# A two-layer kernel: new step orders in its first layer, and an opening with the weights' product and the first projection ahead

## The chip, the cores and the metric

The kernel runs on one core of a Trainium2 chip. The metric is the device time of one execution in microseconds (us); a run's figure is that of one execution, and several runs are summed up by their median.

The core has five engines that run side by side and meet through semaphores: TensorE (PE) multiplies matrices into PSUM banks, VectorE (DVE) and ScalarE (ACT) work on PSUM and SBUF, GpSimd (POOL) works on SBUF and issues gathers and scatters, SyncE (SP) issues plain DMAs. Each engine does its instructions in the order in which they are written.

## The reference

2048 tokens of width 128 pass through two layers. Layer 0 adds to x an attention through hashed buckets and a mixture of experts in which each token goes to one of eight; layer 1 adds a gated delta-rule attention with two convolutions, and a mixture in which each token goes to two of eight. Both halves of a layer read the same normalised x.

```python
xn = _layernorm(x)
x = x + attn0(xn) + ffn0(xn)
xn = _layernorm(x)
x = x + attn1(xn) + ffn1(xn)
# attn0: Q, K, V = heads(Wq), heads(Wk), heads(Wv)
projK = einsum('bhtd,dp->bhtp', K, planes_T)
logitsK = einsum('bhtlk,kr->bhtlr', tanh(projK) / scale, protos_T)
probsK = softmax(logitsK)
bucket_K, bucket_V = probsK.T @ K, probsK.T @ V
out = softmax(Q @ bucket_K.T / sqrt(dim)) @ bucket_V   # then Wo, bo
```

## The kernel before, in words

**Steps and lists.** The work is cut into named steps. `order_one()` makes one list, ONE, for layer 0, and `order_two()` one, TWO, for layer 1. Every engine walks the same list and does its own share of each step; `late()` shifts some kinds of steps back by a few places for one engine (the tables LATE). So a step's place in the list sets its order on PE, DVE, ACT, POOL and SP at once.

**Layer 0.** Attention is done in eight blocks b of 256 tokens. For a block, PE does `proj` (K's hash projection, L704; ACT takes its tanh), `lmm` (the logits, in two halves i, L729; DVE takes the maximum per group, L1155, and subtracts it, L1160), ACT does `exp`, DVE `fin` (sum, L1166, and reciprocal, L1168) and POOL the product with it (L1767). One round later, by the list ROUND, come `bucket` (L741), `sc` (scores, two halves, L760; DVE takes their maximum, L1185, and writes it negated, L1191), `turn`, `mt` (that maximum turned, L771; DVE adds it to q, L1197), `pair` (scores again, transposed, L782; ACT takes exp), `av` (L793), `half`, `norm` and the output product. `kv` and `q` (L718; DVE copies q, L1147, every second block) make K, V and Q.

The mixture of experts works on 23 tiles of 128 sorted rows: `x0` (SP fetches rows and weights), `h0` (PE turns the rows, L692), `g0` (first product, L826 and L831; ACT's tanh, DVE's product with it, L1258), `y0` (second product, L839; DVE scales it, L1129, and SP stores it). `weighted()` merges these into the attention's list: it gives each attention step a weight from SHARE and places an expert step whenever its share of the weight has passed. Rows get to their expert by `ds` (dispatch: DVE works out the places from the router's choice, L1061 to L1083), `scatter` (POOL, 16 indirect DMAs, L1750, into a buffer that SP has zeroed, L549) and come back by `back0` (POOL, 16 gathers, L1784). The last block's steps and the gathers follow the list LAST; `mom`, `ln1` and `rt` there are the next layer's normalisation, transposes and router.

**PSUM.** Eight banks. lmm, sc and pair take two of three double banks each, g0 takes one; so a step of these waits until the readers of an earlier one are done. `plan_banks` fixes who gets which.

**The opening.** SP loads x in four DMAs and then zeroes the sorted buffer in six. ACT issues eleven DMAs of weights and constants, takes the square root of the variances (L1558), and copies the transposed x from PSUM (L1562). DVE makes the moments of four groups of tokens, then waits for the roots, inverts them (L1103) and normalises (L1033). PE waits for all loads of the semaphore d_wa, transposes (L656), does the router (L666), then `wp` (the product of Wk and the planes, L687), then walks ONE, which begins with proj(0) and ds.

```python
w.wait_ge(d_wa, WA_ALL)              # PE, L678
for c in range(4):
    layernorm("ln0", c, 0)
    if c:
        router(0, rw, "ln0", (c - 1,))
router(0, rw, "ln0", (3,))
step = ("wp",)
```

**Layer 1.** HEAD lists its beginning: projections (`pj`, L883), SP's 64 `stack` DMAs (L630: shifted copies of V, four per stack(c,i), two buffers for c = 0 to 3), `gr` (L917), then the convolutions `fl(c)` (L899) and `fs(c)` (L907), which read stack c; a buffer is filled again once fs(c-2) has read it (`w.wait_ge(psum.full(("fs", c - 2)))`). Then come the recurrence (`r0`, `r1`, `rs`, `ro`, eight steps n, two halves u, L870) and 39 expert tiles (`g1`, L998; `y1`, L1006 and L1007) side by side; the gates in four parts m (`ga`, `ht`, `hid` on PE, L863 and L973, then `lg`, `pr`, `cb`, `nm`), which PLAN['gates'] and PLAN['width'] place; and at the end `back1`: 32 gathers on POOL (L1757), each added by DVE (L1135), through four buffers, merged with the rest of the list after PLAN['back']. A gather on POOL also waits for the last `ro` before it in the list.

Of the kernel before, what the change touches and what calls it, by code (L numbers as in the profile page):

```python
# [129 lines left out]
LAST = ([('back0', 0), ('back0', 1), ('back0', 5), ('back0', 2), ('back0', 3), ('back0', 4), ('back0', 7), ('back0', 6), ('bucket',), ('turn',),  # L130
        ('mom', 0), ('sc', 0), ('sc', 1), ('wc', 0)] + [('back0', n) for n in range(8, 12)] + [('mt',), ('mom', 1), ('ln1', 0), ('pair', 0), ('wc',
        1)] + [('back0', n) for n in range(12, 16)] + [('av', 0), ('rt', 1, 0), ('ln1', 1), ('mom', 2), ('wc', 2), ('rt', 1, 1), ('pair', 1),
        ('ln1', 2), ('av', 1), ('rt', 1, 2), ('half', 0), ('half', 1), ('norm',), ('mom', 3), ('ln1', 3), ('rt', 1, 3)])

HEAD = ([('pj', 1, 0), ('ds', 1)] + [('scatter1', n) for n in range(0, 32)] + [('pj', 1, 1), ('pj', 1, 2), ('pj', 1, 3), ('lh', 1), ('l2', 1),
        ('pj', 0, 1), ('pj', 2, 1), ('beta',), ('pj', 0, 0), ('pj', 0, 2), ('pj', 0, 3), ('kb',), ('lh', 0), ('l2', 0), ('pj', 2, 0), ('pj', 2, 2),
        ('pj', 2, 3)] + [('stack', 0, n) for n in range(0, 4)] + [('stack', 1, n) for n in range(0, 4)] + [('qq',), ('mix',), ('vh',)] + [('gr', n)
        for n in range(0, 8)] + [('din',)] + [('sub', n) for n in range(2, 16)] + [('dout',)])
# [16 lines left out]
def order_one():  # L155

    attn = [("proj", 0), ("ds", 0)]
    for a in range(NB + 1):
# [1743 lines left out]
```

## Time and profile before

| | us |
|---|---|
| three runs | 692.17, 696.11, 697.80 |
| median | 696.11 |
| the profiled execution | 695.66 |
| its span in the profile | 693.9 |
| PE, DVE, ACT, POOL busy | 525.5, 449.6, 208.9, 190.8 |
| layer 0's rounds | about 62 to 319 |
| end of layer 0 (gathers, last block) | about 320 to 369 |

All times of the trace are counted from the start of the span. PE's busy time includes what the pipeline hides; a wait is the idle time of an engine ahead of an instruction, with the engine and line that ended it.

### The profile page before, as it was taken

The numbers are of one execution on the slowest core, as the hardware profiler recorded it, in microseconds if no ns is written. First come the engines' busy times: TensorE is split into PE (matmuls) and PEld (weight loads), VectorE is DVE, ScalarE is ACT, GpSimd is POOL, SyncE is SP. The second block draws the span as 40 slices with busy tenths as digits, with TensorE's granted clock in tenths as the row PEclk, the third lists the DMA queues.
The fourth block names the chain that finished last, engine by engine and source line by source line (L and its number), as shares of the span: only waits on it lengthen the run. The fifth ranks groups of instructions, "written<-read, shape, count | busy, mean of one in ns | idle before, by whom it ended". The sixth has DMA issues, their size and how long they took to land.

```text
span 693.9 us, 17843 instructions
## 1 busy us (share of the span) xinstructions
PE 525.5 (76%) x7491; PEld 359.3 (52%) x7491; DVE 449.6 (65%) x925; ACT 208.9 (30%) x374; POOL 190.8 (27%) x145
## 2 busy tenths in 40 slices
PE   3753698887988788885488998785788789787652
PEld 3531565665756666564244445224777667643422
DVE  6596659595957767792547787990254445828945
ACT  2231144435343434442031441101122233424121
POOL 1184040404021302225831776100000000117641
PEclk9975599999989999999576999996699999997755
DMA  8365022413232332301210114440265665401121
GB/s 239 96 176 168 0 83 64 122 54 107 61 102 77 94 97 65 113 9 21 34 16 1 45 48 122 114 128 21 75 188 174 190 182 159 146 22 43 52 53 30
DMA packets 80975, 62.26 MB, mean 90 GB/s; under 512 B 10080, under 2 KB 74368, under 8 KB 80896
## 3 DMA queue, kind: packets, MB, share of 16 engines
q1 hardware_dynamic: 68832, 51.06, 25.7%
q0 software_dynamic: 4864, 6.30, 3.9%
q10 hardware_dynamic: 7200, 3.77, 1.9%
q8 instruction: 59, 0.97, 0.6%
q14 instruction: 20, 0.16, 0.1%
HBM read 44.10 MB, written 12.32 MB: 81 GB/s over the span
## 4 chain that ended last, share of the span: by engine, by line
PE 39%; DVE 19%; issue 9%; SPq 8%; DMA 5%; POOL 5%; ACT 4%; DVEq 0%; ACTq 0%; POOLq 0%
PE ps L883 6%; SPq L630 4%; PE ps L831 4%; POOL X L1784 4%; DVE small L1155 3%; DVE small L1185 3%; DVE BIG L1160 3%; DMA BIG<-in_wd 3%; PE ps L998 3%; PE ps L782 2%; PE ps L729 2%; DMA BIG<-ys,small 2%; PE ps L839 2%; PE ps L863 1%; SPq L588 1%
## 5 line engine op out<-in xcount | busy, mean ns | idle before, releaser
L1767 POOL TENSOR_TENSOR BIG<-BIG,small 128x2048 f32<-128x2048 f32 x16 | 59.0, 3685 | 204.3 <-DVE small L1168 204.0
L1750 POOL DMA_INDIRECT xs<-BIG,small x48 | 51.9, 1082 | 34.8 <-DVE small L1083 21.0
L1809 POOL TENSOR_TENSOR BIG<-BIG 128x512 f32<-128x512 f32 x4 | 4.8, 1212 | 161.1 <-DVE BIG L1478 161.1
L831 PEld LDWEIGHTS ps<-BIG 128*128 128x128 f32 x368 | 46.5, 198 | 3.7 <-issue 0.6
L831 PE MATMUL ps<-BIG 128*128 128x128 f32 x368 | 46.3, 281 | 0.0
L998 PE MATMUL ps<-BIG 128*128 128x128 f32 x312 | 44.0, 286 | 2.9 <-issue 1.4
L1185 DVE TENSOR_REDUCE small<-ps 128x8 f32<-128x1024 f32 x32 | 37.6, 1217 | 12.9 <-PE ps L760 12.9
L883 PE MATMUL ps<-XT,BIG 128*128 128x512 f32 x96 | 44.2, 620 | 0.0
L1155 DVE TENSOR_REDUCE small<-ps 128x64 f32<-128x1024 f32 x32 | 38.9, 1216 | 7.2 <-PE ps L729 7.2
L1757 POOL DMA_INDIRECT BIG<-ys,small x32 | 31.9, 997 | 41.4 <-DMA ys<-BIG 28.6
L998 PEld LDWEIGHTS ps<-BIG 128*128 128x128 f32 x312 | 39.9, 200 | 3.8 <-issue 1.9
L1160 DVE TENSOR_TENSOR BIG<-ps,small 128x1024 f32<-128x1024 f32 x32 | 39.2, 1225 | 1.1
L1620 ACT ACTIVATE BIG<-ps 128x1024 f32<-128x1024 f32 x32 | 31.0, 1021 | 23.1 <-PE ps L782 23.1
L760 PE MATMUL ps<-BIG 32*128 32x256 f32 x256 | 21.2, 450 | 22.0 <-DVE small L1185 11.0
L1724 ACT ACTIVATE BIG<-ps 128x256 f32<-128x256 f32 x39 | 15.0, 384 | 73.1 <-PE ps L998 73.0
L1166 DVE TENSOR_REDUCE small<-BIG 128x128 f32<-128x2048 f32 x16 | 36.4, 2277 | 0.0
L1129 DVE TENSOR_SCALAR BIG<-ps 128x128 f32<-128x128 f32 x62 | 17.6, 284 | 28.1 <-PE ps L1007 18.3
L1527 DVE SCALAR_TENSOR_TENSOR BIG<-BIG,ps 128x256 f32<-128x256 f32 x39 | 16.3, 419 | 27.9 <-ACT BIG L1724 27.9
L899 PE MATMUL ps<-BIG 128*32 128x512 f32 x256 | 28.3, 593 | 7.4 <-DMA BIG<-BIG 7.4
L1596 ACT ACTIVATE BIG<-BIG 128x1024 f32<-128x1024 f32 x32 | 32.1, 1052 | 0.6 <-DVE BIG L1160 0.6
L1020 DVE STREAM_TRANSPOSE BIG<-BIG 128x512 f32<-128x512 f32 (+2 forms) x25 | 27.2, 1105 | 6.7 <-ACT BIG L1659 5.7
L1640 ACT ACTIVATE BIG<-ps 128x512 f32<-128x512 f32 x23 | 13.7, 598 | 58.2 <-PE ps L831 58.2
(254 smaller groups left out, 1113.3 us busy)
## 6 DMA issues: line engine op xcount, KB each, us to landing
BIG<-in_w SPq DMA_DIRECT2D x23, 512.0 KB, 3.7
BIG<-in_w SPq DMA_DIRECT2D x23, 256.0 KB, 3.8
BIG<-in_wg SPq DMA_DIRECT2D x39, 128.0 KB, 2.2
BIG<-in_wu SPq DMA_DIRECT2D x39, 128.0 KB, 2.6
BIG<-in_wd SPq DMA_DIRECT2D x39, 128.0 KB, 2.7
BIG<-BIG SPq DMA_DIRECT2D x64, 71.4 KB, 2.1
ys<-BIG SPq DMA_DIRECT2D x62, 64.0 KB, 2.2
xs<-BIG SPq DMA_DIRECT2D x14, 256.0 KB, 7.6
```

Of the source, the lines that this page charges most:

```text
L831: t = e.matmul(bank(step)[:, i:i + 128], WT[j % NWT][:, o + i:o + i + 128], XsT[j % 2], start=False, stop=(i == 384))
L883: t = e.matmul(bank(s)[:, :], WC[:, v, j, :], XT[:, 2 * c:2 * c + 2, j:j + 256], start=(j == 0), stop=(j == 3))
L998: t = e.matmul(bank(s)[:, i:i + 128], WT[(NTL[0] + j) % NWT][:, i:i + 128], XsT[(NTL[0] + j) % 2], start=True, stop=True)
L1155: own.after(e.tensor_reduce(MX[v], x, AX, ALU.max))
L1160: e.tensor_tensor(o, x, bc_last(MX[v], 16), ALU.subtract).then_inc(s_empty(step), 1)
L1166: own.after(e.tensor_reduce(zz[i], P[n % 3].rearrange("p (l r) -> p l r", r=16), AX, ALU.add))
L1185: e.tensor_reduce(M16[i][:, 8 * v:8 * v + 8], unit(step).rearrange("p (h s) -> p h s", s=128), AX, ALU.max).then_inc(s_empty(step), 1)
L1596: e.activation(p, p, ACT.Exp).then_inc(exp_done, 1)
L1620: e.activation(ET[2 * u + v], unit(step), ACT.Exp, scale=ISQ8).then_inc(s_empty(step), 1)
L1750: e.indirect_dma_start(XSd[L], bass.IndirectOffsetOnAxis(ap=posi[:, 16 * k + n:16 * k + n + 1], axis=0), xn[:, n, :], None).then_inc(d_sca ...
L1757: e.indirect_dma_start(GA[idx % 4], None, YSd[L], bass.IndirectOffsetOnAxis(ap=posi[:, 16 * k + n:16 * k + n + 1], axis=0)).then_inc(d_ga[ ...
L1767: e.tensor_tensor(v, v, bc_last(zz[i], 16), ALU.mult).then_inc(p_ready, 1)
```

## The change

It reorders steps and rebuilds the opening; what each step computes stays, but for the root of the variance, which is one `pow` of -0.5 on POOL where ACT's Sqrt and DVE's reciprocal stood.

```diff
- 'DVE2': {'nm': 1, ..., 'back1': 4, ..., 'lg': 1, ..., 'y1': 1, ...},
+ 'DVE2': {'nm': 2, ..., 'back1': 6, ..., 'lg': 2, ..., 'y1': 2, ...},
 ROUND:
-        ('q', 0, 1), ('mt', 1), ('fin', 0, 0), ...
+        ('mt', 1), ('q', 0, 1), ('fin', 0, 0), ...
-SHARE = {'lmm': 0.3, 'proj': 4, 'turn': 0.6, 'av': 0.3, 'kv': 4, 'fin': 1.5, 'exp': 1.5, 'sc': 1.5}
+SHARE = {'lmm': 1, 'proj': 4, 'turn': 0.6, 'av': 0.3, 'kv': 4, 'fin': 0.6, 'exp': 4, 'sc': 2.5, 'q': 1, 'bucket': 0.3}
 LAST:
-  ..., ('back0', 6), ('bucket',), ('turn',), ('mom', 0), ('sc', 0), ...
-  ('mt',), ('mom', 1), ('ln1', 0), ('pair', 0), ('wc', 1), back0 12 to 15, ('av', 0), ('rt', 1, 0), ('ln1', 1),
-  ('mom', 2), ('wc', 2), ('rt', 1, 1), ('pair', 1), ...
+  ..., ('back0', 6), ('mom', 0), ('bucket',), ('turn',), ('sc', 0), ...
+  ('mt',), ('mom', 1), ('pair', 0), ('ln1', 0), ('wc', 1), back0 12, 14, 15, ('av', 0), ('rt', 1, 0), ('ln1', 1),
+  ('mom', 2), ('back0', 13), ('rt', 1, 1), ('wc', 2), ('pair', 1), ...
 HEAD:
+  ('stack', 1, 2) behind ('pj', 2, 1), ahead of the other seven of stack 0 and 1
 PLAN:
- 'gates': (23, 41, 48),
- 'width': (19, 15, 11),
+ 'gates': (23, 42, 48),
+ 'width': (19, 15, 14),
 order_one:
-    attn = [("proj", 0), ("ds", 0)]
+    attn = [("proj", 0)]
+            if a == 0 and (name, *rest) == ("lmm", 0):
+                attn += [("ds", 0)]
 plan_banks:
+    psum.plan(("wp",), 5)
-    psum.plan(("wp",), 0)
 SP:
+            e.dma_start(wqT, ...)   # then wkv, woT, bo_b: on d_w0
+            w.wait_ge(d_wa, WA_ALL)
             clear(0)
-            w.wait_ge(d_w0, W0_ALL)
 PE:
-            w.wait_ge(d_wa, WA_ALL)
+            w.wait_ge(d_wp, WP_ALL)
             w.wait_ge(xt_pad, 1)
-            for c in range(4): ... transposes and router
             step = ("wp",)
             e.matmul(bank(step)[:, :], wkN, BPl, ...)
+            layernorm("ln0", 0, 0)
+            project(("proj", 0))
+            for c in range(1, 4):
+                layernorm("ln0", c, 0)
+                router(0, rw, "ln0", (c - 1,))
+            router(0, rw, "ln0", (3,))
+            for s in ONE[1:]:
 DVE:
-            for c in range(4): moments(c)
-            for c in range(4): reciprocal, normalise(XN0, c)
+            for c in range(5):
+                if c < 4: moments(c)
+                if c: normalise(XN0, c - 1)
 ACT (DMAs: ident, wkN, BPl on d_wp; misc, rw; cst; PB):
-            for c in range(4): ACT.Sqrt
-            transposes 0 to 3; isc; wp
+            wp; transpose 0; tanh(("proj", 0)); isc; transposes 1 to 3
 POOL:
+            rstd(0, 1) ... rstd(3, 4)   # e.tensor_tensor(rs[:, sl], rs[:, sl], mhalf, ALU.pow)
             w.wait_ge(d_c, C_ALL)
```

Merged with the new weights, the lists of three rounds read as follows between sc(·,1) and the second pair (before, then after); x0, on SP alone, is left out.

```
round 2   sc1,1 exp2,1 q1,1 y3 mt1 fin2,0 g4 pair1,0 proj3 h5 fin2,1 y4 pair1,1
          sc1,1 exp2,1 y3 g4 mt1 q1,1 h5 fin2,0 pair1,0 proj3 y4 fin2,1 pair1,1
round 3   sc2,1 y6 exp3,1 g7 mt2 fin3,0 h8 pair2,0 proj4 y7 fin3,1 g8 pair2,1
          sc2,1 g7 exp3,1 h8 mt2 fin3,0 pair2,0 proj4 y7 g8 fin3,1 pair2,1
round 5   sc4,1 exp5,1 y13 mt4 fin5,0 g14 pair4,0 proj6 h15 fin5,1 y14 pair4,1
          sc4,1 y13 exp5,1 g14 mt4 h15 fin5,0 pair4,0 proj6 y14 fin5,1 pair4,1
```

At the end of layer 1 the lists read (before, then after):

```
rs5,0 g37 h38 hid1,0 rs5,1 y36 g38 hid1,1 ro5,0 y37 y38 ro5,1 back0 lg1 back1 r06,0 ...
rs5,0 g37 h38 ht1 rs5,1 y36 g38 ro5,0 y37 y38 hid1,0 ro5,1 back0 hid1,1 back1 r06,0 ...
```

## Rows read from the trace of the kernel before

**Rows 1.** Windows: us, busy PE, PEld, DVE, ACT, POOL, clock, DMA, GB/s.
```profile
104.90:140.10 35.20, 29.92 (x316) 21.73 (x316) 25.53 (x36) 14.99 (x24) 7.37 (x2) 1.00 0.28 85
...
618.00:624.00 6.00, 2.67 (x74) 1.32 (x68) 1.19 (x3) 0.28 (x1) 2.50 (x3) 1.00 0.16 42
...
642.00:648.00 6.00, 4.32 (x78) 4.06 (x78) 5.69 (x22) 0.97 (x4) 3.21 (x4) 0.50 0.17 44
```

**Rows 2.** Waits of PE, 72 to 320: us in total, times, longest.
```profile
PE ps L760 <- DVE BIG L1160: 6.8, 4, 2.8
...
PE ps L771 <- DVE BIG L1191: 4.1, 3, 1.5
...
PE ps L771 <- DVE BIG L1147: 2.5, 2, 1.3
PE ps L782 <- DVE BIG L1197: 2.5, 3, 0.9
```

**Rows 3.** Opening in order of time: start, us, engine line, [idle before <-releaser].
```profile
11.26 0.78 PEld L656 LDWEIGHTS ps<-ident,BIG 128*128 128x128 f32 x4 [11.26 <-DMA BIG<-in_PB]
11.29 2.28 PE L656 MATMUL ps<-ident,BIG 128*128 128x128 f32 x8 [11.29 <-DVE BIG L1033]
...
21.54 2.06 PE L687 MATMUL ps<-BIG 128*128 128x512 f32 x2
...
22.46 0.28 DVE L1120 TENSOR_TENSOR small<-ps,BIG 128x128 f32<-128x128 f32 x1
...
24.28 3.78 PE L704 MATMUL ps<-XT,BIG 128*128 128x256 f32 x8 [0.69 <-ACT BIG L1577]
...
28.31 0.42 DVE L1061 TENSOR_TENSOR_SCAN KV<-cst,ps 128x128 f32<-128x128 f32 x1 [3.38 <-PE ps L676]
...
31.87 1.17 POOL L1750 DMA_INDIRECT xs<-BIG,small  x1 [8.68 <-DVE small L1083]
...
47.05 3.93 DVE L1231 TENSOR_SCALAR BIG<-BIG 96x128 f32<-96x128 f32 x1
47.20 3.69 POOL L1767 TENSOR_TENSOR BIG<-BIG,small 128x2048 f32<-128x2048 f32 x1
...
58.52 3.67 POOL L1767 TENSOR_TENSOR BIG<-BIG,small 128x2048 f32<-128x2048 f32 x1 [2.19 <-DVE small L1168]
...
62.24 3.64 PE L741 MATMUL ps<-BIG 128*32 128x256 f32 x32 [15.84 <-POOL BIG L1767]
```

**Rows 4.** End of layer 1 in order of time, columns as in rows 3.
```profile
606.48 1.02 PE L863 MATMUL ps<-XT,BIG 128*128 128x512 f32 x2
...
609.05 1.02 PE L973 MATMUL ps<-BIG 128*128 128x512 f32 x2
...
616.91 0.39 PE L1007 MATMUL ps<-BIG 128*128 128x128 f32 x2
...
620.90 0.99 POOL L1757 DMA_INDIRECT BIG<-ys,small  x1 [28.64 <-DMA ys<-BIG]
```

**Rows 5.** DMA issues by line: KB each, median us from issue to landing.
```profile
cst<-in_cst ACTq DMA_DIRECT2D x1, 204.0 KB, 3.7
```

**Rows 6.** Groups by line: busy, mean ns of one, idle before.
```profile
L1155 DVE TENSOR_REDUCE small<-ps 128x64 f32<-128x1024 f32 x32 | 38.9, 1216 | 7.2 <-PE ps L729 7.2
L1160 DVE TENSOR_TENSOR BIG<-ps,small 128x1024 f32<-128x1024 f32 x32 | 39.2, 1225 | 1.1
```

**Rows 7.** End of layer 0 in order of time, columns as in rows 3.
```profile
352.82 1.63 POOL L1777 TENSOR_TENSOR small<-small 128x4 f32<-128x4 f32 x1
...
354.21 1.15 PE L782 MATMUL ps<-BIG 32*128 32x256 f32 x16
```

**Rows 8.** Chain that ended last, around fs(0) and fl(1); timeline row of fl(1) last.
```profile
438.37 0.59 SPq L630
438.96 0.34 issue
...
441.34 7.08 PE L899 MATMUL ps<-BIG 128*32 128x512 f32 x64 [2.29 <-DMA BIG<-BIG]
```

**Rows 9.** A later projection in order of time, columns as in rows 3.
```profile
87.71 2.00 PE L704 MATMUL ps<-XT,BIG 128*128 128x256 f32 x8
```

More of the change, by code:

```diff
@@ L130 @@
[L130 to L133, printed above, removed]
+SHARE = {'lmm': 1, 'proj': 4, 'turn': 0.6, 'av': 0.3, 'kv': 4, 'fin': 0.6, 'exp': 4, 'sc': 2.5, 'q': 1, 'bucket': 0.3}
@@ new lines @@
+LAST = ([('back0', 0), ('back0', 1), ('back0', 5), ('back0', 2), ('back0', 3), ('back0', 4), ('back0', 7), ('back0', 6), ('mom', 0), ('bucket',),
+        ('turn',), ('sc', 0), ('sc', 1), ('wc', 0)] + [('back0', n) for n in range(8, 12)] + [('mt',), ('mom', 1), ('pair', 0), ('ln1', 0), ('wc',
+        1), ('back0', 12), ('back0', 14), ('back0', 15), ('av', 0), ('rt', 1, 0), ('ln1', 1), ('mom', 2), ('back0', 13), ('rt', 1, 1), ('wc', 2),
+        ('pair', 1), ('ln1', 2), ('av', 1), ('rt', 1, 2), ('half', 0), ('half', 1), ('norm',), ('mom', 3), ('ln1', 3), ('rt', 1, 3)])
@@ L1542, in _ @@
             w = Waits(e)
[L1543 to L1544 removed]
+            e.dma_start(ident[:, :], io["ident"]).then_inc(d_wp, 16)
+            e.dma_start(wkN, io["wkN"]).then_inc(d_wp, 16)
+            e.dma_start(BPl, io["BPl"]).then_inc(d_wp, 16)
             e.dma_start(misc[:, 0:32], io["misc"]).then_inc(d_wa, 16)
             e.dma_start(rw, io["rw"]).then_inc(d_wa, 16)
[L1547 to L1548 removed]
+            e.dma_start(cst[:, 0:408], io["cst"]).then_inc(d_c, 16)
             e.dma_start(PB, io["PB"]).then_inc(d_wa, 16)
[L1550 to L1558 removed]
             def transposed(step, c):
@@ L1569, in sorted_in, with tanh @@
                 e.activation(XsT[J % 2], bank(s)[:, 0:128], ACT.Copy).then_inc(s_empty(s), 1)
-            for c in range(4):
-                transposed(("ln0", c), c)
-            w.wait_ge(d_wa, WA_ALL)
-            e.activation(isc[:, 0:1], lt_b, ACT.Exp).then_inc(isc_ready, 1)
+            def tanh(s):
+                b = s[1]
+                for gg in range(2):
+                    step = s + (gg,)
+                    w.wait_ge(psum.full(step))
+                    if b:
+                        w.wait_ge(psum.full(("lmm", b - 1, 1, 1)))
+                    e.activation(TH[:, 2 * gg:2 * gg + 2, :], bank(step)[:, :].rearrange("p (g t) -> p g t", g=2), ACT.Tanh).then_inc(s_empty(step), 1)
             step = ("wp",)
@@ L1577, in _ @@
             e.activation(Wproj.rearrange("p (g q n) -> p q g n", g=4, q=4), bank(step).rearrange("p (q g n) -> p q g n", q=4, g=4), ACT.Copy).then_inc(s_empty(step), 1)
-            for s in late(ONE, LATE["ACT1"]):
+            transposed(("ln0", 0), 0)
+            tanh(("proj", 0))
+            w.wait_ge(d_wa, WA_ALL)
+            e.activation(isc[:, 0:1], lt_b, ACT.Exp).then_inc(isc_ready, 1)
+            for c in range(1, 4):
+                transposed(("ln0", c), c)
+            for s in late(ONE[1:], LATE["ACT1"]):
                 k = s[0]
                 if k == "proj":
-                    b = s[1]
-                    for gg in range(2):
-                        step = s + (gg,)
-                        w.wait_ge(psum.full(step))
-                        if b:
-                            w.wait_ge(psum.full(("lmm", b - 1, 1, 1)))
-                        e.activation(TH[:, 2 * gg:2 * gg + 2, :], bank(step)[:, :].rearrange("p (g t) -> p g t", g=2), ACT.Tanh).then_inc(s_empty(step), 1)
+                    tanh(s)
                 elif k == "kv":
```

93 lines of the change are left out of this document (44 added, 49 removed).

## The prediction

> **What bounds the kernel now.** I read the windows by stage first, because no engine is full over the whole span. A round of layer 0 (from one bucket step to the next) lasts 35.2 us; PE is busy for 29.9 us of it and DVE for 25.5 [rows 1]. Neither is the limit alone: the loss is PE standing while DVE finishes something. So the waits of PE over the seven rounds come second [rows 2]. The reader is to see there that PE's longest waits stand ahead of sc (L760, for the PSUM banks that lmm's subtraction, L1160, frees) and ahead of mt (L771, for sc's maximum, L1191, and for a copy of q, L1147: 4.1 + 2.5 us), and 2.5 us ahead of pair (L782, for mt's addition, L1197). Third is the opening in order of time [rows 3]: PE stands for 15.84 us before the first bucket step at 62.24, and GpSimd ends that wait. Last is the end of layer 1 [rows 4]: GpSimd's 32 gathers of expert rows start at 620.90, after a wait for the last stored tile, and the chain of the end runs behind them.
>
> **Opening.** Removed: four Sqrt on ACT and four reciprocals on DVE; added: four `pow` on GpSimd. Moved: the product wp and proj(0) go ahead of the router, dispatch (ds) goes behind lmm(0,0), and four weight DMAs go from ACT's queue to SP's, ahead of the six zeroing DMAs. Before, PE starts at 11.26, held by PB, the seventh DMA of ACT's queue [rows 3]. After, it needs only ident, wkN and BPl, that queue's first three. BPl has 256 KB and would be issued at about 1.7; the 204 KB of cst, issued second before, took 3.7 us to land [rows 5], so I take 1.7 + 4.1 = 5.8 for PE's start.
> From there: wp 2.1; the transposes and the router 10.3 (11.29 to wp's start at 21.54 before); proj(0) 3.8, and 0.7 for the copy of XT that it waits for [rows 3]. That is 16.9 us, so the router ends near 22.8, against some 21.6 before. The first maximum and the count take 2.5 (22.46 to 24.93). Now lmm(0,0) stands ahead of ds in DVE's order: two tiles of 1.22 + 1.23, 4.9 us [rows 6]. Then dispatch, 3.6 us to the first scatter (28.31 to 31.87) [rows 3]. Sum: 22.8 + 2.5 + 4.9 + 3.6 = 33.8, against 31.87: the scatters start 1.9 us later.
> What is queued behind them on GpSimd sets the first bucket. Twelve scatters take 31.87 to 47.20, then come the product of fin(0,0), 3.69, and four scatters, and fin(0,1) starts at 58.52, having waited 2.19 us for DVE [rows 3]. DVE now reaches fin(0,1) 2 to 3 us earlier, since its idle 3.38 us before dispatch are filled with lmm(0,0). So the 1.9 us eat most of the 2.19 us of waiting, and the bucket stays at about 62.2: **0 us**, although proj(0) is ready 10 us earlier. From both sides: -4 if every landing is earlier than taken, +3 if PE starts at 8.
> The new `pow` is costed by the one ahead of layer 1, 1.63 us [rows 7]; it lies beside wp. One row speaks against it: a 96x128 tensor_scalar of DVE that met a GpSimd product ran for 3.93 us and ended with it [rows 3]. The Trainium skill (SBUF — State Buffer, section Who interferes with whom) has it that a DVE operation in a two-port mode and a GpSimd operation lock each other out for a whole instruction. The row agrees; by that rule each of the four normalisations could wait for one `pow`, and the first would start 1 us later: the sum would be +1 in place of 0. I keep 0: 0.3 us of the waiting are left, and the +3 covers the rest.
>
> **Rounds.** The shares of SHARE decide between which attention steps the expert steps (h, g, y) fall. By the old shares the part from lmm(b,0) to mt holds about half of the weight, by the new ones two thirds (exp 4 in place of 1.5, sc 2.5, fin 0.6). Merging the lists by hand, I find: in rounds 2, 5 and 7 one g more stands before mt; in round 1 g(0) moves ahead of sc(0,1) and y(0) ahead of pair; in rounds 4 and 6 little moves, in 3 nothing that counts. In even rounds the second q now follows mt, so its copy no longer precedes mt's addition on DVE, and it covers the wait ahead of pair.
> In prices: the waits ahead of mt, 4.1 + 2.5 = 6.6 us, go; of the 6.8 ahead of sc I take 1, in round 1. What is late next: in rounds 5 and 7 pair has no g between mt and itself, 0.5 us each; in round 7 g(22) no longer covers the wait ahead of norm, 0.7. Moved work also passes through DVE: g's product with the gate now precedes mt's addition (0.69 us) in three rounds, but PE's g stands beside it. Sum: -6.6 - 1 + 1.0 + 0.7 = -5.9; I take **-5**. Bounds: -9 (PE idle another 3 us shorter) and +2 (DVE, 26 of 35 us, makes each wait reappear elsewhere).
>
> **End of layer 0.** back0(13) moves behind mom 2, pair(7,0) ahead of ln1(0). Pair 0 gains 3 us, but av, rt and ln1(1) follow in order and rt(1,1) now waits for XT ahead of wc 2: pair(7,1), at 354.21 [rows 7], comes at about 354. **0**, bounds -1 and +1. The GpSimd queue gets its third `pow` one gather earlier; nothing waits for that.
>
> **Head of layer 1.** Four of the 64 stack DMAs, stack(1,2), move 28 issues earlier on SP. That shortens the issue line by 4 x 0.63 = 2.5 us (0.59 and 0.04 between), and fl(1), which waits 2.29 us, can start at once. But stack 2 may not overwrite its buffer before fs(0) has read it, and SP already stands there, 0.34 us at 438.96 [rows 8]. So fl(2) and fl(3) come when they came: **0**, bounds -2.5 and 0.
>
> **End of layer 1.** PLAN moves gates of part 1 by one recurrence step: both hid(1,*) leave the expert stage and follow y1(38). Each is 3.6 us of PE (606.48 to 610.07 the first, the second alike) ahead of the last tile's product, which ends at 617.30 [rows 4]. Without them y1(38) must still wait for its own gate chain on ACT and DVE, about 1.5 us that hid hid; so 7.2 - 1.5 = 5.7 us earlier. The first gather also waits for ro(5,1), now behind hid(1,0): 3.6 us of PE against 3.6 us of store, landing and issue (617.30 to 620.90), so they run beside each other. The hids go where PE is idle: it is busy for 2.67 of the 6 us before 624 [rows 1]. Gathers and the chain behind them come 5 to 6 us earlier; DVE's back steps are put two places later, which can hold a gather whose buffer is not free. I take **-5**, bounds -8 and 0.
>
> **Sum.** The profiled execution is 695.66 us (span 693.9 and 1.8 around it); the runs' median, 696.11, is 0.45 above it. 695.7 + 0 - 5 + 0 + 0 - 5 = 685.7, so **686**.
>
> **Rivals.** (a) The end of layer 1 gives its gain back: POOL and DVE pace the gathers, not their start. For it: DVE is busy for most of that stage (5.69 of 6 us after 642 [rows 1]); against: ro and the gathers move together. 691; chance 0.13. (b) The rounds gain nothing, because DVE in its order bounds the first half: 691; 0.12. (c) Neither gains: the change doesn't do what it says, 696; 0.08. (d) Slower: dispatch behind lmm(0,0) is not paid for. If PE starts at 8 or later, the scatters start after 36, GpSimd's chain has no wait left to absorb it, bucket(0) comes after 65, and every expert tile and round follows; with the rounds' +2, 700 to 704; it decides from a router end of 25 on. 0.07. (e) The opening gains: at 24.28 eight matmuls of proj took 3.78 us, and at 87.71, at the upper level of the clock, 2.00 [rows 3, 9]. If the longer unbroken stretch brings the upper level (2.4 GHz in place of 1.2) before proj(0), proj and the router shrink from 13.2 to some 7 us, but fin(0,1) on DVE then bounds: 682; 0.05. The Trainium skill (TensorE: Matmul & The Clock Gate, section Part 1) has sustained activity lift the clock; here the stretch from 11.3 to 28 never got there, so I give it little. The forecast itself has 0.55, with 680 to 692 as its own range.
>
> **Numbers.** 677 is the forecast with both gains near their ends, 697 the case without gains; outside lie (d) and the far ends, under 2 in 10. One per cent, about what a measurement of this kernel can tell from no change, is 7 us: faster means under 689.1. The forecast gives 0.45 of its 0.55 to that, (e) 0.05, (a) and (b) together 0.09: 0.59. Slower is (d), 0.07; the rest, 0.34, is within.
>
> **What would show it.** Right: the first scatter at 33 to 35 and bucket(0) at 61 to 64; PE's waits for L1191 and L1147 under 2 us over the rounds; a round near 34.5; fl(1) without a wait, fl(2) with one; the first gather 9 to 16 us earlier in the span (the 5 of the rounds included). Wrong: a first scatter after 36; new waits ahead of pair or sc as long as those that went; gathers that start early and end at the old distance from the stage's start plus what was won; or a stretch at the lower clock where there was none.

## The result, and the profile after

The changed kernel took 673.57 us (median of four runs, 668.88 to 679.80) where the kernel before took 695.63: the ratio is 0.9665, interval 0.9595 to 0.9734. It is the ratio of the means of the fast runs, and the run of 679.80 was in a slower state and is left out. Two later sets of runs gave 0.9697 (0.9668 to 0.9725) and 0.9757 (0.9715 to 0.9799). So the change wins 2.4 to 3.4%, 17 to 23 us; the forecast was 10. The sign was right, and so were the places but for the opening, which was put at 0; three of its terms were too small, all on the same side.

The profiled execution is the fastest of the four, 668.88 us with a span of 667.1, so its stages add up to more than the median's gain: 693.9 - 667.1 = 26.8 us. By stages, from the starts of the steps in both traces: to bucket(0) 62.24 became 56.51 (-5.7); first round 42.68 became 39.07 (-3.6); rounds 2 to 7 214.25 became 205.13 (-9.1); end of layer 0 51.02 became 51.31 (+0.3); from there to the recurrence 134.83 became 135.15 (+0.3); from the recurrence's start to the last tile's product 111.89 became 104.17 (-7.7); the rest 76.99 became 75.76 (-1.2).

The opening after, in order of time (start, us, engine line, then the idle time and its releaser), which answers to [rows 3]; L689 is wp, L700 proj, L673 the router, L1770 a scatter, L1787 the product of fin, L1244 a step of the expert biases (L1231 before), L754 bucket:

```profile
6.22 2.08 PE L689 MATMUL ps<-BIG 128*128 128x512 f32 x2 [6.22 <-DMA BIG<-in_BPl]
...
8.09 1.06 PE L661 MATMUL ps<-ident,BIG 128*128 128x128 f32 x4
...
9.93 1.97 PE L700 MATMUL ps<-XT,BIG 128*128 128x256 f32 x8 [0.78 <-ACT XT L1566]
...
15.03 2.51 PE L673 MATMUL ps<-BIG,XT 128*128 128x8 f32 x16
...
28.32 1.20 POOL L1770 DMA_INDIRECT xs<-BIG,small  x1 [11.06 <-DVE small L1096]
...
38.70 0.25 DVE L1244 TENSOR_SCALAR BIG<-BIG 96x128 f32<-96x128 f32 x1
...
44.09 3.69 POOL L1787 TENSOR_TENSOR BIG<-BIG,small 128x2048 f32<-128x2048 f32 x1
...
52.76 3.70 POOL L1787 TENSOR_TENSOR BIG<-BIG,small 128x2048 f32<-128x2048 f32 x1
...
56.51 3.64 PE L754 MATMUL ps<-BIG 128*32 128x256 f32 x32 [16.20 <-POOL BIG L1787]
```

The reader is to see two things. proj(0) takes 1.97 us, as a later projection does [rows 9], not 3.78 [rows 3]: TensorE runs at its upper level (2.4 GHz) here and ran at the lower one (1.2 GHz) before. And GpSimd's second product follows its last scatter with no wait, where it had waited 2.19 us for DVE; the bias instruction of DVE took 0.25 us in place of 3.93.

Rounds 2 to 7 as one window, before and then after (us; busy PE, PEld, DVE, ACT, POOL; granted clock, DMA share, GB/s), and the fourth round alone, before and after:

```profile
104.92:319.17 214.25, 180.50 (x1899) 133.28 (x1898) 159.04 (x214) 89.57 (x140) 44.22 (x12) 0.98 0.26 77
175.35:214.69 39.34, 34.77 (x336) 25.44 (x334) 26.98 (x39) 15.65 (x24) 7.37 (x2) 0.91 0.31 94
```

```profile
95.58:300.71 205.13, 176.35 (x1899) 131.08 (x1898) 159.46 (x214) 88.87 (x140) 44.14 (x12) 1.00 0.27 81
164.33:199.34 35.01, 31.69 (x335) 23.49 (x333) 27.00 (x38) 15.42 (x24) 7.33 (x2) 1.00 0.35 106
```

PE does the same 1899 matmuls. Its idle time falls from 33.75 to 28.78 us, which is 5.0; its busy time falls by 4.2, of which 3.1 lie in the fourth round, whose granted clock was 0.91 before. In the first round, before and after, the idle time stays (8.0 and 7.9 us) and the busy time falls by 3.5, at a granted clock of 0.73 and 0.86:

```profile
62.24:104.92 42.68, 34.69 (x302) 24.55 (x302) 23.74 (x31) 14.73 (x23) 7.37 (x2) 0.73 0.27 83
```

```profile
56.51:95.58 39.07, 31.17 (x302) 22.14 (x302) 22.82 (x30) 14.83 (x23) 7.37 (x2) 0.86 0.34 108
```

The waits of PE in rounds 2 to 7 after the change (us in total, times, longest; L773 is sc, L784 mt, L795 pair, L839 g's first product, L821 norm, L742 lmm):

```profile
PE ps L773 <- DVE BIG L1173: 4.3, 4, 1.5
PE ps L839 <- DVE BIG L1173: 3.8, 4, 1.2
...
PE ps L821 <- DVE BIG L1223: 2.5, 4, 1.0
PE ps L795 <- DVE BIG L1210: 2.5, 3, 0.9
...
PE ps L784 <- DVE BIG L1204: 1.7, 2, 1.1
...
PE ps L742 <- DVE small L1198: 0.7, 1, 0.7
```

### The profile page after: what moved, and what is told of

Its sections match the earlier page's. It is cut to its first block, busy times and chain, and to the rows that moved or that the text cites. A ratio compares the mean times of both kernels' runs of the same rounds, so it can differ in the third digit from the quotient of the medians.

```text
span 667.1 us, 17838 instructions
## 1 busy us (share of the span) xinstructions
PE 517.6 (78%) x7491; PEld 353.5 (53%) x7491; DVE 445.2 (67%) x921; ACT 205.9 (31%) x369; POOL 194.6 (29%) x149
## 3 DMA queue, kind: packets, MB, share of 16 engines
q1 hardware_dynamic: 69408, 51.39, 26.8%
## 4 chain that ended last, share of the span: by engine, by line
PE 47%; DVE 17%; issue 10%; POOL 6%; DMA 4%; ACT 4%; SPq 3%; DVEq 0%; ACTq 0%; POOLq 0%
PE ps L896 7%; PE ps L844 5%; PE ps L1011 4%; POOL X L1801 4%; PE ps L912 4%; DVE small L1168 3%; DVE small L1198 3%; DVE BIG L1173 3%; DMA BIG<-in_wd 3%; PE ps L883 2%; PE ps L852 2%; PE ps L742 2%; PE ps L795 2%; PE ps L1019 2%; PE ps L930 2%
## 5 line engine op out<-in xcount | busy, mean ns | idle before, releaser
L1787 POOL TENSOR_TENSOR BIG<-BIG,small 128x2048 f32<-128x2048 f32 x16 | 58.9, 3687 | 189.1 <-DVE small L1181 189.0
L1770 POOL DMA_INDIRECT xs<-BIG,small x48 | 51.0, 1062 | 37.2 <-DVE small L1096 23.3
L1011 PEld LDWEIGHTS ps<-BIG 128*128 128x128 f32 x312 | 40.9, 204 | 3.9 <-ACT BIG L1573 3.1
L1777 POOL DMA_INDIRECT BIG<-ys,small x32 | 32.5, 1016 | 33.6 <-PE ps L883 22.6
L773 PE MATMUL ps<-BIG 32*128 32x256 f32 x256 | 19.3, 417 | 21.0 <-DVE small L1198 11.3
L1540 DVE SCALAR_TENSOR_TENSOR BIG<-BIG,ps 128x256 f32<-128x256 f32 x39 | 16.3, 417 | 28.3 <-ACT BIG L1733 28.3
L912 PE MATMUL ps<-BIG 128*32 128x512 f32 x256 | 31.2, 643 | 4.0 <-DMA BIG<-BIG 4.0
L896 PEld LDWEIGHTS ps<-XT,BIG 128*128 128x128 f32 x96 | 19.0, 200 | 23.8 <-issue 23.8
```

The source lines that it names most:

```text
L896: t = e.matmul(bank(s)[:, :], WC[:, v, j, :], XT[:, 2 * c:2 * c + 2, j:j + 256], start=(j == 0), stop=(j == 3))
L912: t = e.matmul(bank(s[:2])[32 * i:32 * i + 32, :], LG[:, i, g, :], x, start=(g == 0), stop=(g == 7))
L1011: t = e.matmul(bank(s)[:, i:i + 128], WT[(NTL[0] + j) % NWT][:, i:i + 128], XsT[(NTL[0] + j) % 2], start=True, stop=True)
L1770: e.indirect_dma_start(XSd[L], bass.IndirectOffsetOnAxis(ap=posi[:, 16 * k + n:16 * k + n + 1], axis=0), xn[:, n, :], None).then_inc(d_sca ...
L1777: e.indirect_dma_start(GA[idx % 4], None, YSd[L], bass.IndirectOffsetOnAxis(ap=posi[:, 16 * k + n:16 * k + n + 1], axis=0)).then_inc(d_ga[ ...
L1787: e.tensor_tensor(v, v, bc_last(zz[i], 16), ALU.mult).then_inc(p_ready, 1)
```

## The experiments

In some sets of runs the kernel before took 695 to 696 us, in others 708 to 713; so kernels are compared by their ratio to the kernel before of the same set.

**The four parts, each alone on the kernel before.** The opening:

```diff
 kernel before, with plan_banks, SP, PE, DVE, ACT, POOL and ds of the change;
 LATE, ROUND, SHARE, LAST, HEAD, PLAN as before
```

> The kernel before with the new opening alone (places of dispatch, wp, proj(0), the four pow, the weight DMAs). Theory 1 (the opening is worth what bucket(0) shows, 62.24 before and 56.51 after, and the first round gains besides because more of it runs at the upper level of the clock: 42.68 before, 39.07 after): bucket(0) near 56.5, the first round near 39, 6 to 9 us faster, 687 to 690. Rival (the earlier bucket is given back in the rounds, because the expert tiles come no earlier): bucket(0) near 56.5, the second bucket near 104, 694 to 696.

Measured: 0.9960 (0.9924 to 0.9996). bucket(0) came at 59.52 where both expected 56.5: this execution's proj(0) took 3.75 us, and its first scatter went out at 31.31. The first round took 40.9 and the second bucket came at 100.39, between the two expectations, as the time does.

The rounds:

```diff
-SHARE = {'lmm': 0.3, ..., 'exp': 1.5, 'sc': 1.5}
+SHARE = {'lmm': 1, ..., 'fin': 0.6, 'exp': 4, 'sc': 2.5, 'q': 1, 'bucket': 0.3}
 ROUND:
-  ('q', 0, 1), ('mt', 1), ...
+  ('mt', 1), ('q', 0, 1), ...
```

> The kernel before with the new SHARE and ROUND alone. Theory 1 (shorter waits of PE ahead of mt, sc and pair, by order alone): the seven rounds take 250 to 252 us in place of 256.9, the time is 689 to 691. Rival (most of what the rounds won after the change, 244.2 against 256.9, is the clock: 9 us of the low level fewer in them, won by the opening or by chance): the rounds at the upper level stay at 35.2 us, 694 to 696.

Measured: 0.9895 (0.9825 to 0.9965), 687.07 us. All seven rounds took 244.93 us, less than theory 1 had, and rounds 2 to 7 of them 205.08, as in the changed kernel, all at the upper level. The rival falls: the order does it, not the opening. Not all of it shows in the time, because from the last bucket step to the end this execution took 378.7 us against 374.7.

The end, PLAN and LATE:

```diff
-  'gates': (23, 41, 48), 'width': (19, 15, 11)
+  'gates': (23, 42, 48), 'width': (19, 15, 14)
-  'DVE2': {'nm': 1, 'back1': 4, 'lg': 1, 'y1': 1, ...}
+  'DVE2': {'nm': 2, 'back1': 6, 'lg': 2, 'y1': 2, ...}
```

> The kernel before with the new PLAN and LATE alone (gates of part 1 a step later, width 14, DVE's back steps later). Theory 1 (the hidden products behind the last tile's product let the gathers start 6 to 7 us earlier and the end follows): first gather near 614, end of the span 686, 687 to 690. Rival (it gives the gain back, DVE and POOL pacing the gathers): first gather near 614, end of the span 691 to 694.

Measured: 0.9901 (0.9864 to 0.9937), 687.67 us; the first gather at 613.32, the span 684.5. Theory 1 holds.

LAST and HEAD:

```diff
 LAST: ('mom', 0) ahead of bucket, ('pair', 0) ahead of ('ln1', 0), ('back0', 13) behind ('mom', 2), ...
 HEAD: ('stack', 1, 2) behind ('pj', 2, 1)
```

> The kernel before with the new LAST and HEAD alone. Theory 1 (nothing: stack 2 waits for fs(0), pair(7,1) comes as late as before): 695 to 697, fl(1) without its wait of 2.29 us and fl(2) with one. Rival (the shorter line of stack issues passes on to the end): 692 to 693.5.

Measured: 0.9993 (0.9953 to 1.0032). fl(1) waited 0.15 us where it was 2.29, fl(2) 4.18 where it was 2.20. The product of the four ratios is 0.9751, against 0.9665, 0.9697 and 0.9757 for the whole: the parts add up within their intervals.

**The opening: what starts the scatters, and what sets bucket(0).** The changed kernel once more:

> The changed kernel once more, beside the three that follow. If the opening's gain depends on when TensorE's matmuls reach the upper level of the clock (proj(0) at 9.93 took 1.97 us in the profile of after, at 10.81 it took 3.75 in the kernel with the new opening alone), this execution's first scatter lies at either 28.3 or 31.3 and its bucket(0) at 56.5 or 59.5; if the opening is fixed by its order, at 28.3 and 56.5 again. 670 to 676.

Measured: 0.9697; first scatter 30.14, bucket(0) 58.37, proj(0) 3.75 us and the matmuls at the upper level from about 15 us on. So the same order gives either: the level rose before 9.93 in one execution and between 13.2 and 15.2 in this one.

With wp and proj(0) behind the router:

```diff
 PE and ACT:
-  wp; transposes 0; proj(0); transposes 1 to 3 and router
+  transposes 0 to 3 and router; wp; proj(0)
```

> The changed kernel with wp and proj(0) back behind the router on PE and ACT, all else of the opening as changed. Theory 1 (wp, the transposes and proj(0) ahead bring the upper level, transposes and router alone do not, as before the change): the transposes of four take 1.06 to 1.09 us each and proj(0) near 3.8, the first scatter lies at 33 or later, bucket(0) at 60 to 62, 677 to 680. Rival (PE's start at 6 to 7 us does it, whatever runs first): the level rises within 4 to 8 us, proj(0) takes 2.0, the first scatter at 29 to 31, 673 to 676.

Measured: 0.9724 (0.9686 to 0.9761). Theory 1's mechanism is there in full; PE's rows of this kernel (L661 transposes, L696 proj, L753 bucket):

```profile
7.39 1.16 PE L661 MATMUL ps<-ident,BIG 128*128 128x128 f32 x4 [7.39 <-DVE BIG L1045]
...
14.77 1.09 PE L661 MATMUL ps<-ident,BIG 128*128 128x128 f32 x4
...
21.67 3.78 PE L696 MATMUL ps<-XT,BIG 128*128 128x256 f32 x8 [0.69 <-ACT BIG L1590]
...
63.47 2.79 PE L753 MATMUL ps<-BIG 128*32 128x256 f32 x24 [16.57 <-POOL BIG L1786]
```

PE started at 7.39 and was busy without a gap from 10 to 20 us, and all of it ran at the lower level; the first scatter went out at 35.25 and bucket(0) at 63.47, later than before the change and than the 60 to 62 expected. Of the 5 us between this bucket and that of the changed kernel in the same set, 2.5 us show in the time (689.51 against 687.01), within the intervals.

With dispatch ahead of lmm(0,0), as before the change:

```diff
-    attn = [("proj", 0)]
+    attn = [("proj", 0), ("ds", 0)]
...
-            if a == 0 and (name, *rest) == ("lmm", 0):
-                attn += [("ds", 0)]
```

> The changed kernel with dispatch ahead of lmm(0,0), as before the change. Theory 1 (GpSimd's 16 scatters and two products, 28 us without a gap, set bucket(0), so every us that the scatters start earlier is a us won, and lmm(0,0) on DVE loses nothing since DVE stands from 50.9 to 62.5): first scatter 24 to 25, bucket(0) 52 to 53, 4 us faster than the changed kernel, 667 to 671. Rival (lmm(0,0) and the two fin behind it come later by dispatch's 3.6 us and set the bucket): bucket(0) at 56 to 60, as the changed kernel or slower.

Measured: 0.9681 (0.9641 to 0.9721), no different from the changed kernel. The first scatter did go out at 25.96, but bucket(0) came at 57.87. The rows say why (L1242 is the bias step's instruction that is L1244 above, L1785 the product of fin, L752 bucket):

```profile
42.86 3.68 POOL L1785 TENSOR_TENSOR BIG<-BIG,small 128x2048 f32<-128x2048 f32 x1 [1.75 <-DVE small L1179]
43.10 3.52 DVE L1242 TENSOR_SCALAR BIG<-BIG 96x128 f32<-96x128 f32 x1
...
54.14 3.68 POOL L1785 TENSOR_TENSOR BIG<-BIG,small 128x2048 f32<-128x2048 f32 x1 [2.20 <-DVE small L1179]
...
57.87 3.64 PE L752 MATMUL ps<-BIG 128*32 128x256 f32 x32 [13.12 <-POOL BIG L1785]
```

GpSimd now waits for DVE twice, 1.75 and 2.20 us, and DVE's small instruction met the product and ended with it. It is the picture of before the change [rows 3]. Splitting the scatters does not help while that stands:

```diff
-                attn += [("experts", 0)] + [("scatter", n) for n in range(12)]
+                attn += [("experts", 0)] + [("scatter", n) for n in range(11)]
...
-                attn += [("scatter", n) for n in range(12, NT)]
+                attn += [("scatter", n) for n in range(11, 14)]
+            elif a == 0 and (name, *rest) == ("fin", 1):
+                attn += [("scatter", n) for n in range(14, NT)]
```

> As the kernel before it, and the scatters are split 11, 3, 2 around the two products of fin(0,*) in place of 12, 4 and none. Theory 1: the products start when DVE has their sums, near 38.5 and 46.2, bucket(0) at 50 to 51, the last scatter ends near 52.5 as in the changed kernel, so the first expert rows are fetched no later: 6 us faster than the changed kernel, 665 to 669. Rival (the first expert tile then holds PE: its transposed rows stand in the list behind the first sc and come from the last scatter): bucket(0) at 50 to 51, the second bucket no earlier than in the kernel with dispatch ahead alone, 667 to 671.

Measured: 0.9675 (0.9642 to 0.9708), bucket(0) at 57.48: fin(0,1)'s product started at 53.76 and had waited 3.47 us for DVE, whose tensor_scalar took 3.52 again. Both expectations missed the cause. So, back with 12 scatters and with dispatch still ahead, the bias step was put later on DVE, behind fin(0,1) and lmm(1,0):

```diff
-LATE = {'DVE1': {'bias': 1, 'av': 2},
+LATE = {'DVE1': {'bias': 8, 'av': 2},
```

> The changed kernel with dispatch ahead of lmm(0,0) and the bias step on DVE behind fin(0,1). Theory 1 (in the kernel with dispatch ahead alone, DVE's tensor_scalar of the bias step met GpSimd's product of fin(0,0), took 3.52 us in place of 0.25, and held fin(0,1)): that instruction lies behind both products or in a gap and fin(0,1) is ready near 46, GpSimd's chain of 28 us sets the bucket again, bucket(0) at 54 to 56, 3 us faster than the changed kernel. Rival (fin(0,1) is held by the exponentials or by DVE's other work): bucket(0) at 57 to 58, no gain on the changed kernel.

Measured: 0.9654 (0.9602 to 0.9705); bucket(0) at 58.06, outside theory 1's 54 to 56, because in this execution the upper level didn't come in the opening (proj(0) 3.75, transposes 1.09 to the last) and the first scatter went out at 29.29. From there GpSimd's chain took 28.8 us, as theory 1 has it. The second product no longer waits for DVE; 1.22 us of idle time stand ahead of the first, which starts 0.1 us behind fin(0,0)'s reciprocal on DVE. The bias step now meets the second product, where no GpSimd product waits for it (L1242 is its instruction, L1785 the product):

```profile
53.85 4.25 DVE L1242 TENSOR_SCALAR BIG<-BIG 96x128 f32<-96x128 f32 x1
...
54.31 3.70 POOL L1785 TENSOR_TENSOR BIG<-BIG,small 128x2048 f32<-128x2048 f32 x1
```

Next, 13 scatters ahead of fin(0,0), one behind it and two behind fin(0,1). The bias step stands between fin(0,1) and lmm(1,0) here, one step ahead of its place in the run before, so this run differs from it in two things:

```diff
-LATE = {'DVE1': {'bias': 1, 'av': 2},
+LATE = {'DVE1': {'bias': 5, 'av': 2},
...
+                attn += [("experts", 0)] + [("scatter", n) for n in range(13)]
...
+                attn += [("scatter", n) for n in range(13, 14)]
+            elif a == 0 and (name, *rest) == ("fin", 1):
+                attn += [("scatter", n) for n in range(14, NT)]
```

> As the kernel before it, and 13 scatters stand ahead of fin(0,0)'s product, one between the products and two behind. Theory 1: bucket(0) at 51 to 53, the last scatter ends near 54 as in the changed kernel, 5 to 7 us faster than the changed kernel, 0.960 to 0.963 of the time before. Rival (expert rows, fetched behind the last scatter, hold the first h on PE, which stands 5 to 6 us behind the bucket): bucket(0) at 51 to 53 and a new wait ahead of the first h, the second bucket no more than 3 us earlier than in the changed kernel, 0.965 to 0.968.

Measured: 0.9679 (0.9635 to 0.9724), though bucket(0) came at 49.41. The second bucket came at 93.01. The rows (L1248 is another instruction of the bias step, L773 the first sc):

```profile
45.24 4.34 DVE L1248 CAST BIG<-BIG 96x384 bf16<-96x384 f32 x1
45.67 3.69 POOL L1787 TENSOR_TENSOR BIG<-BIG,small 128x2048 f32<-128x2048 f32 x1
49.41 3.64 PE L754 MATMUL ps<-BIG 128*32 128x256 f32 x32 [4.40 <-POOL BIG L1787]
...
58.11 2.09 PE L773 MATMUL ps<-BIG 32*128 32x256 f32 x16 [5.06 <-DVE BIG L1173]
```

The rival's effect came, by another cause than it named: not the expert rows but lmm(1,*) on DVE, which stood behind the bias step, held the first sc for 5.06 us. Two rounds also had a stretch at the lower level (160 to 164 and 293 to 297) and took 1.6 us longer each. The last step, all else as in this kernel, puts the bias behind lmm(1,0) again:

```diff
-LATE = {'DVE1': {'bias': 5, 'av': 2},
+LATE = {'DVE1': {'bias': 8, 'av': 2},
```

> The kernel with both, with the bias step on DVE three places later still, behind lmm(1,0) and fin(0,1). Theory 1 (the 9 us of the earlier first bucket were lost because the bias step, 4.3 us of it against GpSimd's product, stood ahead of lmm(1,*) whose subtraction the first sc waits for, 5.06 us): bucket(0) at 49 to 53, that wait under 2 us, the second bucket 3 us or more earlier than in the kernel with both, 0.957 to 0.964 of the time before. Rival (the first round is set by PE at the lower level of its clock and by the expert rows): second bucket as in the kernel with both, 0.966 to 0.970.

Measured: 0.9566 (0.9536 to 0.9595), 667.53 us. The first sc waits 1.14 us, for ACT, as theory 1 has it:

```profile
59.57 2.09 PE L773 MATMUL ps<-BIG 32*128 32x256 f32 x16 [1.14 <-ACT BIG L1614]
```

Its places were missed. The upper level didn't come in this opening either, the first scatter went out at 29.77, bucket(0) came at 54.79, and the second bucket at 93.33, as the rival had it. The first round took 38.54 us where it was 43.60, at a granted clock of 0.79 and 0.75; the shorter wait is 3.9 us of that, and whether the rest is the clock is not separated. The two kernels were not run in one set. Beside the changed kernel in one set:

> The changed kernel, beside the version with dispatch ahead, the scatters split 13, 1, 2 and the bias step behind lmm(1,0), on the same chip. Theory 1 (the gain is the same 3.0 to 3.4% on every chip, and the other version's lead of about 1% is real): 0.966 to 0.970. Rival (the lead was the chip's): 0.957 to 0.960, as the other version.

> The version with the bias step behind lmm(1,0), once more, on the same chip as the changed kernel. Theory 1: 0.955 to 0.960, 1% faster than the changed kernel, because the second bucket comes 3 to 5 us earlier and nothing of it is given back behind. Rival: within 0.3% of the changed kernel.

Measured: 0.9757 (0.9715 to 0.9799) for the changed kernel and 0.9629 (0.9585 to 0.9673) for this version, 690.10 and 683.21 us: the ratios are 1.3% apart, with intervals that don't meet. Theory 1 of both holds in the lead. Neither ratio lies where theory 1 put it; the changed kernel's was nearer to the parts' product. Second buckets: 94.37 and 91.50, 2.9 us apart where 3 to 5 were expected; two rounds of the changed kernel's execution held a short stretch at the lower level, 3.2 us in all, and none of the other's. This version is faster than both kernels; that is shown for its three moves together (dispatch, scatters, bias step), not for each.

**The rounds: SHARE or ROUND.**

```diff
 kernel before, with ROUND alone: mt ahead of the second q
```

> The kernel before with the new ROUND alone (the second q behind mt); SHARE stays as before. Theory 1, as forecast: the 2.5 us of waits ahead of mt for q's copy go and nothing else: the rounds take 254 us in place of 256.9, 0.996. Rival (that swap alone brings what SHARE and ROUND brought together, by taking away PE's pause before the stretch at the lower level in the fourth round): the fourth round at 35 to 36 in place of 39.3 and no lower level in it, the rounds 248 to 250, 0.990.

Measured: 1.0018 (0.9980 to 1.0057). Neither. The wait ahead of mt for q's copy went, and the one for the scores' maximum took its place; the first row of PE's waits in its rounds, where it was 4.1 before [rows 2]:

```profile
PE ps L771 <- DVE BIG L1191: 8.1, 5, 2.4
```

```diff
 kernel before, with SHARE alone
```

> The kernel before with the new SHARE alone; ROUND stays as before. Theory 1 (SHARE alone carries what SHARE and ROUND won together; ROUND alone won nothing): the rounds take 245 to 249 us in place of 256.9, 0.988 to 0.991. Rival (it needs the swap of the second q and mt, whose wait for q's copy stays otherwise): 250 to 253, 0.993 to 0.997.

Measured: 0.9885 (0.9842 to 0.9928). Rounds 2 to 7 took 205.11 us, the same as with both: SHARE carries all of it. (All seven took 241.2, its first round 36.0 at a granted clock of 0.91.)

**The end: PLAN or LATE.**

```diff
 kernel before, with PLAN alone: 'gates': (23, 42, 48), 'width': (19, 15, 14)
```

> The kernel before with the new PLAN alone; LATE stays as before. Theory 1 (the end's gain of 7 us is the place of the two hid behind the last tile's product, LATE adds nothing): first gather near 613, 0.990 of the time before, 687 to 689 on a chip where the kernel before takes 695. Rival (without the later back steps on DVE the gathers are held and the gain is halved): 0.994 to 0.997.

Measured: 0.9959 (0.9929 to 0.9989), first gather at 627.72. That spoke for the rival, but in another set of runs than PLAN with LATE; so both once more, in one set:

> The kernel before with the new PLAN and LATE, once more, beside PLAN alone on the same chip. Theory 1 (PLAN carries it, the difference between 0.990 and 0.996 was the chips'): both within 0.3% of each other. Rival (LATE is needed, because DVE's adds otherwise stand ahead of work that PE waits for): this one 0.990, the other 0.995 or more.

> The kernel before with the new PLAN alone, once more. Theory 1: within 0.3% of the kernel with PLAN and LATE. Rival: 0.5% or more slower than it.

Measured: 0.9883 (0.9852 to 0.9914) with LATE, 0.9937 (0.9909 to 0.9965) without. The rival's numbers came, twice with nearly the same distance, 0.58 and 0.54%. Both times the intervals overlap, so a gain of LATE is likely and not shown. From the recurrence's start to the last tile's product the two took 105.4 and 109.8 us, from there to the end 76.1 and 77.6; in the first pair the same stretch took 106.9 with LATE and 106.5 without. What both pairs have in it: PE waits 3.2 us for DVE's product with the gate (L1531) without LATE and 2.0 with it. Beyond this 1.2 us, how LATE does it stays open: waits for a tile's weights (in_wd) vary between 6.6 and 13.2 us from one execution to the next and cover it.

## Why the prediction was right and where it was wrong

**Opening: forecast 0, shown 3 to 6 us at bucket(0) and 2.8 us in the time of that part alone.** Right: PE's start (5.8 forecast, 5.93 to 7.10 in the traces), the price of lmm(0,0) ahead of ds (4.9 forecast, 4.2 between the first scatters at 30.14 and, without it, 25.96), and GpSimd's chain behind the first scatter (62.2 - 33.8 = 28.4 forecast; 28.2 in all executions of the changed kernel). One step failed, and it carries the number: "router 10.3 and proj(0) 3.8" took over durations of the lower level. The router was through at 17.5 in the profiled execution and at 19.4 in the second, where 22.8 was forecast. The kernel with the router first shows that sum come true: PE started 1.6 us later than forecast, and the first scatter came at 35.25 (33.8 + 1.6 = 35.4). With wp and proj(0) in front the level rose in the opening in eight of ten executions, and in those of them with dispatch where the change puts it the first scatter came at 28.3 to 31.3. This was rival (e), at 0.05 far too cheap: its counter-argument, a stretch before the change that never got there, was a stretch of transposes and router matmuls, other work than the new one. What (e) saw behind it did not come: fin(0,1) on DVE bounded nothing.

A second step gave the right number by luck. The forecast had the wait of 2.19 us ahead of fin(0,1) go, because the scatters start later and DVE's idle time before dispatch is filled. The wait went though the scatters started earlier. Its cause stood in the same group [rows 3], the 3.93 us of a tensor_scalar beside GpSimd's product, and I used that row for the `pow` alone. In the changed kernel lmm(0,0) is done ahead of dispatch, so DVE is through the bias step before the first product begins, and the two don't meet. The account closes: in the profile of after 31.87 - 28.32 = 3.55 of the earlier start and the 2.19 of the wait make 5.74, and bucket(0) moved by 5.73; in the second execution 1.73 + 2.19 = 3.92 and 3.87.

**Rounds: forecast -5 over the seven, shown -12.7 in the profile and -7.3 in the time of that part alone.** The idle time of PE fell by 5.0 us in rounds 2 to 7 and by 0.1 in the first, the size that was forecast, and the waits ahead of mt went from 6.6 to 1.7, as forecast. That the sum fits is in part luck: the waits of lmm for sc's maximum fell too (3.7 to 0.7), those of g's first product (1.6 to 3.8), of L821 (1.5 to 2.5) and of av for DVE's scaling (0.8 to 2.0) grew. Nothing in it was due to the swap of mt and q, to which I had put 2.5 us. The step that failed is a term put at nothing without a reason: PE's busy time. It fell by 4.2 us in rounds 2 to 7, for the larger part the stretch at the lower level in the fourth, and by 3.5 in the first, where the granted clock rose from 0.73 to 0.86. I had read the waits of the rounds and the clock of one of them only [rows 1], at 1.00. The first round's share varies: in three executions of the changed kernel it took 39.07, 39.17 and 36.08 us, at 0.86, 0.86 and 0.91.

**End of layer 0 and head: forecast 0, shown 0.** 51.02 and 51.31 us; 134.83 and 135.15. fl(1) starts without a wait and fl(2) with one, as forecast, 4.04 us where it was 2.20 before. It also took 10.03 us itself where it was 7.08, and fl(3) then had no wait where it had 2.88, so the convolutions together took 38.4 us where they took 39.1:

```profile
421.45 7.06 PE L912 MATMUL ps<-BIG 128*32 128x512 f32 x64
...
433.41 10.03 PE L912 MATMUL ps<-BIG 128*32 128x512 f32 x64 [4.04 <-DMA BIG<-BIG]
```

**End of layer 1: forecast -5, shown -7 to -8.** The mechanism was right. The rows (L1020 the last tile's product, L986 hid(1,0), L1777 the first gather), which answer to [rows 4]:

```profile
591.34 0.39 PE L1020 MATMUL ps<-BIG 128*128 128x128 f32 x2
...
594.14 1.02 PE L986 MATMUL ps<-BIG 128*128 128x512 f32 x2
...
596.21 0.99 POOL L1777 DMA_INDIRECT BIG<-ys,small  x1 [22.30 <-PE ps L883]
```

The gather follows the last product by 4.9 us, where it was 4.0, and waits for ro on PE rather than for the stored tile, as the sum had it. Mis-sized were two terms. The 1.5 us taken off for y1(38)'s own gate chain do not show in this profile: from the recurrence's start to the last tile's product 7.7 us went where 5.7 were forecast (over all executions 110.8 to 115.4 us with the old PLAN, 104.1 to 110.5 with the new). And LATE: I held it for a risk, and in both comparisons it came out at about half of the gain, though not clear of the noise. From the first gather to the end the time fell from 73.0 to 70.9 us, so rival (a) falls here. In the sets with the longer times it holds in part: there this stretch took 75.8 us with the old PLAN, 78.6 with the new and 79.2 in the changed kernel.

**The sum and the range.** 0 - 5 + 0 + 0 - 5 became, by the parts alone, -2.8 - 7.3 - 0.5 - 6.9 = -17.5 us of 695. Each lies within the bounds given for its part; in the profile of the changed kernel two lie beyond them, bucket(0) with -5.7 against -4 and the rounds with -12.7 against -9. So two steps failed: the opening's 0, with the router and proj(0) priced at the lower level, and the rounds' -5, a sum of waits with nothing for PE's busy time. The end's -5 was mis-sized. The range followed from them: 677 is little more than the two gains at their ends (695.7 - 9 - 8 = 678.7) and leaves out the opening's -4; all bounds added give 671.2, beside the 673.57 measured. The opening and the rounds share a cause, the clock, so their errors could fall on one side, and the bounds were to be added. By the ratios of the two later sets 695.7 us would be 674.6 and 678.8, so how far the time lies below the range is in part chance. That the whole won 22 us in its first set and the parts 17.5 is within the intervals.

## What to carry to other kernels

When steps are reordered, read the clock of the stretch as well as its waits: which steps stand first can decide whether proj(0) takes 1.97 or 3.78 us. When an engine waits for DVE, look whether one of DVE's small instructions met a long one of GpSimd's on SBUF; moving the bias step by a few places took the 2.20 us ahead of the second product away. And an earlier first step is worth what the step behind it can use: beside the third execution of the changed kernel, 8.9 us won at bucket(0) came to 1.3 at the end of the rounds with the bias step ahead of lmm(1,0) on DVE; with it behind, 5.6 us came to 6.1, of which 3.2 are the other's two stretches at the lower level.

## What the runs showed of the hardware

**The level of TensorE's clock in the opening.** With transposes and router first, none of ten executions had left the lower level when proj(0) began, at 21.7 to 24.3 us (it took 3.51 to 3.78 us there), though PE was busy without a gap before it: 4.70 of 4.70 and 5.50 of 5.50 us in two windows of the kernel before, from 11.30 on. With wp, four transposes and proj(0) first, eight of ten executions reached the upper level, 3.7 to 9.3 us after PE's first matmul; the other two stayed below through all transposes and the router. So the order makes it likely and not certain, and one opening differs from the next by 3 us (first scatters at 28.32 and 31.31). The granted clock of these stretches reads 1.00 at either level, so here only the durations tell. The Trainium skill (TensorE: Matmul & The Clock Gate, section Part 1) has sustained activity lift the clock. The eight executions agree; the kernel before, busy in both windows and still at the lower level, does not, and what in the order makes the difference no run separates.

**A stretch at the lower level that belongs to an order of steps.** All eight executions with the old SHARE show one or two in rounds 2 to 7, and these rounds took 213.8 to 217.2 us; with the new SHARE nine of twelve show none and took 205.1 us each time, and three show two short ones and took 208.3 or 208.4. Windows of the kernel before, around the one in its fourth round:

```profile
190.00:192.00 2.00, 0.94 (x4) 0.28 (x2) 2.00 (x2) 2.00 (x3) 0.00 (x0) 1.00 0.59 150
192.00:194.00 2.00, 1.41 (x11) 1.19 (x11) 1.89 (x5) 0.06 (x1) 0.00 (x0) 1.00 0.83 277
194.00:196.00 2.00, 2.00 (x19) 1.26 (x16) 1.97 (x2) 0.00 (x0) 0.00 (x0) 0.55 0.00 0
```

PE was busy for 0.94 and 1.41 of 2 us while it waited for sc's maximum ahead of mt, and then the granted clock fell to 0.55. The longest wait there is 1.46 us, and the round's busy time was 3.1 us longer than after the change. That the wait causes it is argued from their order in time; no run took the wait away alone.

**DVE and GpSimd.** A tensor_scalar of 96x128 took 0.25 us alone and 3.52, 3.93 and 4.25 beside GpSimd's product; a cast of 96x384 0.36 and 4.34; a tensor_tensor of two SBUF tiles 0.22 and 2.52. Each ended 0.1 to 0.2 us behind the product. In three of these rows, the 3.93, the 4.25 and the 4.34, DVE's instruction starts 0.15 to 0.46 us ahead of the product's row and is held all the same. Reductions of 128x2048 beside it took 2.23 to 2.28, as alone. This agrees with the Trainium skill (SBUF — State Buffer, section Who interferes with whom), by which casts, tensor_scalar and tensor_tensor with both inputs in SBUF can be locked out and reductions are not.

**Sets of runs.** Where the kernel before took 708 to 713 us, the rounds lasted as long as elsewhere (33.4, 35.4, 35.0, 33.1, 33.9 us for rounds 2 to 6 of the changed kernel in both), and the time was lost in the head of layer 1 and at the end: from 351.03 to 492.57, 141.5 us against 135.2, with PE's many 32x32 matmuls of gr waiting 20.6 us for their own issue against 7.8. Why the sets differ is open.
